# A new order on TensorE in the first attention: scores beside the first head outputs, the query projection last

## The reference

```python
q = (layernorm(x) @ Wq.T + bq)          # 16 heads of 16 features
k = (ctx @ Wk.T + bk)
v = (ctx @ Wv.T + bv)
scores = q @ k.T / 4 + attn_mask + 2 * side   # side: 16 heads x 128 x 128 for each tile
x = x + softmax(scores) @ v @ Wo.T + bo
# then: a router of 14 experts on layernorm(x), 2 of them for each token;
# a second attention, a second mixture of experts (8 experts and a shared one)
```

## Time and profile before

| | |
|---|---|
| median of 3 runs | 949.08 us (947.41 to 949.46) |
| the profiled execution | 948.31 us, its span 946.4 us |
| PE busy over the span | 905.2 us, 96% |
| DVE, ACT, POOL busy | 506.1, 497.4 and 439.1 us (53%, 53%, 46%) |
| first attention | from the start to about 181 us of the span |

### The profile page before, as it was taken

How to read it: one execution, slowest core, us unless ns; L and a number is a source line. 1 busy time by engine, 2 the same in 40 slices (tenths; PEclk the granted TensorE clock), 3 DMA queues, 4 the chain that set the end, 5 groups by cost and what they waited for, 6 DMA issues and landing times. The chain is left out here.

```text
span 946.4 us, 25076 instructions
## 1 busy us (share of the span) xinstructions
PE 905.2 (96%) x7324; PEld 813.1 (86%) x7325; DVE 506.1 (53%) x2073; ACT 497.4 (53%) x1409; POOL 439.1 (46%) x572
## 2 busy tenths in 40 slices
PE   5999999798999999879999999999999999999997
PEld 4788888597999999767878899999999999999996
DVE  3988988583444344269999583222433333333332
ACT  3878787333344344379999763344334443344332
POOL 6778876203555555435555250001444444444433
PEclk9999999898999999899999999999999999999999
DMA  9876583943222222344221099201111111111110
GB/s 267 235 238 209 173 252 112 337 151 98 70 72 67 72 72 71 90 164 128 86 74 54 24 329 375 103 31 38 45 55 55 49 55 47 52 46 55 51 34 1
DMA packets 98567, 107.33 MB, mean 113 GB/s; under 512 B 9858, under 2 KB 83992, under 8 KB 98234
## 3 DMA queue, kind: packets, MB, share of 16 engines
q1 hardware_dynamic: 88160, 80.76, 26.5%
q0 software_dynamic: 9936, 25.32, 8.9%
q10 hardware_dynamic: 394, 0.31, 0.1%
HBM read 86.68 MB, written 21.50 MB: 114 GB/s over the span
## 5 line engine op out<-in xcount | busy, mean ns | idle before, releaser
L2171 ACT ACTIVATE hid<-experts_bank,vecT 128x128 f32<-128x128 f32 x492 | 180.4, 367 | 273.9 <-PE experts_bank L2114 243.1
L2124 PE MATMUL experts_bank<-w,hid 128*128 x984 | 227.6, 381 | 0.0
L2124 PEld LDWEIGHTS experts_bank<-w,hid 128*128 128x128 f32 x984 | 180.5, 190 | 23.1
L1756 POOL DMA_INDIRECT rows<-token_rows,src x84 | 82.4, 981 | 155.8 <-DVE dst L1751 93.5
L2114 PEld LDWEIGHTS experts_bank<-Hn 128*128 128x128 f32 x1248 | 145.3, 192 | 2.0
L2114 PE MATMUL experts_bank<-Hn 128*128 128x128 f32 x1248 | 145.5, 275 | 0.0
L2114 PEld LDWEIGHTS experts_bank<-xT,wp 128*128 128x128 f32 x720 | 89.8, 197 | 4.4 <-issue 2.2
L2114 PE MATMUL experts_bank<-xT,wp 128*128 128x128 f32 x720 | 90.1, 280 | 2.0 <-DVE xT L2180 2.0
L2188 DVE COPY Hn<-w 128x1024 f32 x78 | 54.6, 701 | 67.9 <-PE experts_bank L2114 67.5
L2063 POOL DMA_INDIRECT out_dram<-Hn,dst x39 | 45.7, 1172 | 86.8 <-DVE Hn L2211 86.8
L1281 ACT ACTIVATE E<-U,mn 128x128 f32<-128x128 f32 x256 | 79.7, 392 | 2.2 <-DVE mn L1361 2.2
(11 more groups left out here) (279 smaller groups left out, 1494.4 us busy)
## 6 DMA issues: line engine op xcount, KB each, us to landing
w<-in_fside_Bx16xSxS_dram SPq DMA_DIRECT2D x32, 512.0 KB, 4.6
w<-in_L_ffn_w_dram SPq DMA_DIRECT2D x28, 512.0 KB, 6.2
w<-in_L_ffn_Wfc_dram SPq DMA_DIRECT2D x8, 1024.0 KB, 14.0
w<-in_L_ffn_Wproj_dram SPq DMA_DIRECT2D x8, 1024.0 KB, 12.8
y<-token_outputs SPq DMA_DIRECT2D x16, 256.0 KB, 3.4
ctx<-in_ctx_dram SPq DMA_DIRECT2D x26, 128.0 KB, 4.7
keys_values<-WT SPq DMA_DIRECT2D x12, 256.0 KB, 2.0
token_rows<-Hn SPq DMA_DIRECT2D x16, 128.0 KB, 5.6
```

The source lines that it names most:

```text
L1756: pool.indirect_dma_start(out=weights["rows"][:, n % 2], out_offset=None, in_=c["hn"], in_offset=bass.IndirectOffsetOnAxis(ap=routing["src ...
L2124: last = pe.matmul(Y[par][:, 0:D], hid[par][:, f], weights["w2"][:, bass.ds(e * (FC * D) + f * D, D)], start=(f == 0), stop=(f == FC - 1))
L2171: act.activation(hid[par][:, f], HB[f % 4][:, 0:P], moe.act, bias=bias).then_inc(hid_ready, 1)
```

## The change

Three blocks of PE's loop change places; no other engine's program changes. At the head of a pass `turn_e(b-1, 2)` and `turn_out(b-2)` come before `scores(b)`, and `outputs(b-1, 0)` and `outputs(b-1, 1)` directly behind it, ahead of `bring(b+1)`. Further on, `outputs(b-1, 2)` and `outputs(b-1, 3)` come before `project_q(b+1)` instead of behind it.

```diff
             for b in range(-1, B + 3):
+                if has(b - 1):
+                    turn_e(b - 1, 2)
+                if has(b - 2):
+                    turn_out(b - 2)
                 if has(b):
                     scores(b)
                 if b == 0:
                     turn_w(2)
                     project_v(0)
+                if has(b - 1):
+                    outputs(b - 1, 0)
+                    outputs(b - 1, 1)
                 if has(b + 1):
                     bring(b + 1)
                 if has(b - 1):
-                    turn_e(b - 1, 2)
-                if has(b - 2):
-                    turn_out(b - 2)
-                if has(b - 1):
-                    outputs(b - 1, 0)
-                    outputs(b - 1, 1)
                     turn_e(b - 1, 3)
                 if has(b - 2):
                     project_out(b - 2)
-                if has(b + 1):
-                    project_q(b + 1)
                 if has(b - 1):
                     outputs(b - 1, 2)
                     outputs(b - 1, 3)
+                if has(b + 1):
+                    project_q(b + 1)
                 if has(b):
                     turn_e(b, 0)
```

## The result

The changed kernel takes 972.57 us, median of 4 runs (971.59 to 974.25), against 949.06 us before (median of 4 runs, too): a ratio of 1.0239, 95% interval 1.0208 to 1.0270, so 23.5 us slower. The forecast was slower, 965.0 us, with a range of 959.5 to 969.5; the time lies above it. The profiled execution took 971.59 us, span 969.7 us.

A forecast was written before the change was run, and what follows sets the result against it. PE was taken to set the pace, at 9.62 us a tile. Losses of 4.6 + 0.6 + 10.8 = 16.0 us on the profiled 948.31 gave 964.3, plus 0.77 to the median: 965.0 us, range 959.5 to 969.5.

The forecast's parts named there:

- Part 1: turn_out ahead of scores: v_out allows it 2.13 us behind turn_back's start, so PE waits 0.81 us.
- Part 2: outputs 2 and 3 ahead of project_q: outputs(t-1, 3) waits 0.29 us for et_out.
- Part 3: scores and outputs side by side: one array shape change saved, 0 to 0.30 us a tile, buying nothing.
- the drain rule of the Trainium skill: Between scores and outputs: a change of tiling mode drains TensorE; one drain would be left there.
- the gain of one of two changes: Between scores and outputs: one of two drains saved; 0.2 us taken for all such gains together.
- The period: Mid-stage, from one scores to the next: 10.57 us, 0.95 us more than 9.62.
- the walk: Step-by-step timing of one tile through PE and DVE, giving scores 10.57 us apart; 1.5 us uncertainty in the total.
- the sum for the first tiles: Pipeline start: scores(2) 4.6 us late behind turn_out(0), the next tile losing 0.6 us more.
- no fall of the clock was expected: Attention: PE keeps its granted clock, being busy for about 9.4 of 10.57 us.
- one wait of 1.27 us: First tiles before the change: turn_out waited 1.27 us for v_out while the clock was 1.00.
- The rival on the clock: Behind or within the attention, a waiting PE loses its clock more often: 3 us and more, 968 and up; 7%.

The follow-up runs named there:

- v_early: Changed kernel with v_out(t) moved ahead of divide(t-2) on DVE; 960.92 us, ratio 1.0120.
- head_only: Changed kernel with project_q back ahead of outputs 2 and 3, the new head of a pass kept; 969.45 us, ratio 1.0212.
- tail_only: Kernel before with only outputs 2 and 3 moved ahead of project_q, in all tiles; 950.87 us, ratio 1.0021.
- side_by_side: Changed kernel with turn_out moved behind outputs 0 and 1, and project_q back ahead of outputs 2 and 3; 951.11 us, ratio 1.0011.
- after_again: Changed kernel run and profiled once more without an edit; 970.65 us.
- filled: Changed kernel with PE turning the identity (20 and 12 unused transposes) before turn_out in the passes of tiles 2 and 3; 970.01 us, ratio 1.0227.
- new_to4: Changed kernel with the new order only in passes up to b = 4, the old order from b = 5 on; 960.3 us, ratio 1.0121.

## Why the prediction was right in kind and wrong in size

The mechanism was as forecast, step by step. `turn_out` waits for `v_out` (Part 1): 2.12 us from `turn_back` against 2.13, and v_early removes it. `outputs(t-1, 3)` waits for `et_out` once the head is early (Part 2): 0.21 us by head_only against 0.29, and nearly nothing alone (tail_only). The neighbourhood buys nothing (Part 3): side_by_side. On the drain rule of the Trainium skill that was weighed there: the step out of row tiles costs 1.07 us into column tiles as into full ones, which fits a drain; the gain of one of two changes that was drawn from it does not show, as the tiles of side_by_side are 9.65 us apart and not less than 9.62. The period came out at 10.65 against 10.57; the difference is the step from the two transposes of `turn_out` to `scores`, 0.34 us where 0.24 was put. That is a miss of 0.1 us a tile. That 8.19 meets 8.20 is partly luck, as two misses cancel there: `project_q` starts 113.76 - 109.42 = 4.34 us behind `scores` (4.45 in the walk), and takes 114.75 - 113.76 = 0.99 us to the next group, where 0.90 was put.

The step that failed is the sum for the first tiles, 4.6 + 0.6 us, and with it the sentence that in the attention no fall of the clock was expected: it put waits on PE at their own length, at the upper level of the clock. By `scores(4)` the walk allows for at most 4.6 + 0.6 + 0.95 = 6.15 us; 12.3 were lost there, 5.0 of them to the clock. Against before, the profiled execution lost:

| term | forecast | measured | how measured |
|---|---|---|---|
| first weights late | 0 | 1.2 | scores(0) |
| clock rises late | 0 | 2.7 | step 0 to 1: 13.11, in after_again 10.36 |
| order, tile 0 to 2 | 4.6 | 5.0 | 10.36 - 9.12 and 12.16 - 8.44 |
| order, tiles 2 to 4 | 0.6 and part of 10.8 | 1.2 | filled: 11.35 + 10.43 - 20.62 |
| clock falls | 0 | 2.3 | after against filled |
| tiles 4 to 15 | the rest of 10.8 | 11.3 | 11 times 1.03 |
| behind | 0 | -0.3 | end |
| sum | 16.0 | 23.3 | |

The order's own part is 17.4 us, 1.4 over the forecast; 5.0 us are the clock, 1.2 the landing of one matrix. The falls alone would not have left the range: without the 3.9 us of the late start this execution would be at 967.7. The second trace of the changed kernel started early and still took 970.65 us. It stood 10.24 us at the lower level behind its waits, where the first stood 6.83, and GpSimd held DVE twice (last section), with two waits of PE longer by 1.20 and 1.84 us. That hold is a second term that the walk put at nothing; in the profiled execution it happened not to strike. That both end so near to one another is chance. The prediction took its evidence from one wait of 1.27 us with no fall behind it and carried that to waits of 2.4 us and more, which no row showed. The rival on the clock named the right mechanism, with 7%, and put 3 us and more on one loss, where two cost 2.3 us together; so the range ended short of it.

The Trainium skill says, in "TensorE: Matmul & The Clock Gate", A second HAM failure mode: psum-queue depth-cycling, that in a bf16 kernel which cycles through PSUM banks frequent short idling between groups of matmuls makes the clock swing. This trace shows falls in the first tiles, at longer waits (2.37 and 1.42 us); in mid-stage, where short idling recurs, it does not agree: 0.54 us of it in each 10.65 us left the clock at 1.00.

What stays open is whether the late rise at the start (23 to 28 us in four of six profiles with the new order in the first tiles, 13 to 21 us in the other five) is more than chance. PE's program is the same up to that point, and the changed kernel showed both 25.0 and 13.6 us.

## What to carry to other kernels

When an engine that sets the pace runs its program in order, an instruction may be moved ahead only as far as the answer of the other engine allows: follow the ring (here `turn_back`, six DVE instructions, `turn_out`) and compare it with the work that is left in between, here 1.39 us for an answer of 2.12. Walk the first tiles, while the pipeline fills, apart from the steady ones (here they made 12.3 of 23.3 us), and price a wait on TensorE there with the clock that it may lose. If an early place is wanted, move the releaser first: `v_out` ahead of `divide` gave back two thirds of the loss in each tile.

## What the runs showed of the hardware

A small DVE instruction can be held for the length of a GpSimd one. In the second trace of the changed kernel the scaling of four means took 2.13 us, where it took 0.21 us in the first trace, and it ended with GpSimd's addition. DVE's row:

```profile
50.65 2.13 DVE L705 TENSOR_SCALAR nmean<-MV 128x4 f32<-128x4 f32 x1
```

GpSimd's row:

```profile
50.41 2.34 POOL L346 TENSOR_TENSOR w<-w 128x1024 f32<-128x1024 f32 x1
```

50.41 + 2.34 = 52.75 and 50.65 + 2.13 = 52.78. In the first trace DVE came to the same instruction 0.15 us ahead of GpSimd's addition, and was not held:

```profile
53.38 0.21 DVE L705 TENSOR_SCALAR nmean<-MV 128x4 f32<-128x4 f32 x1
```

```profile
53.53 2.35 POOL L346 TENSOR_TENSOR w<-w 128x1024 f32<-128x1024 f32 x1
```

Where DVE was held 1.92 us longer, `turn_out` waited 1.84 us longer, 3.26 instead of 1.42. It is no single case: in nine of the eleven profiles this scaling, or the like step on the four variances next to it, was held so once or twice between 20 and 60 us, eleven times in all, for 0.67 to 2.34 us, and each time it ended 0.02 to 0.04 us behind GpSimd's addition. In head_only, new_to4 and v_early, too, a hold of 2.2 to 2.3 us goes with a wait of 3.3 to 3.4 us before `scores(3)`. In the new order a race of a few tenths of a us thus decides about 1.9 us. The Trainium skill, "SBUF — State Buffer", Terms, describes a pair of ports that DVE and GpSimd take in turn for a whole instruction; these rows fit it. Not every DVE instruction is held: the minima took 0.28 to 0.29 us each beside GpSimd's addition at 47.04 us in the first trace, and no run shows what makes the difference.
